# TensorE's counts of logits, shared products and attended rows behind a drain, and variance's root ahead of the weights' low halves

## The reference

```python
xn = _layernorm(x, axis=-1)
s = _L0_attn_ref(xn, Wq, Wk, Wv, Wo)         # attention over the 256 features of a batch, not over its rows
g = _silu(_L0_ffn_ref(xn, gate_weight, w1, w2, w3, sw1, sw2, sw3))
x = x + s * g
```

## Time and profile before

| what | value |
|---|---|
| time, median of 3 runs | 685.56 us (684.07 to 687.75) |
| the profiled execution's own time | 691.99 us |
| its span | 690.2 us |
| PE busy | 548.6 us (79%), 4095 matmul passes |
| DVE, ACT, POOL busy | 472.2, 359.1, 383.4 us (68%, 52%, 56%) |
| TensorE's granted clock, mean | 0.922 |

### The profile page before, as it was taken

One profiled execution on the slowest core, in us unless ns is written; L12 is line 12 of the kernel. 1 busy time (PEld: TensorE's weight loads), 2 busy tenths in 40 slices (PEclk: granted clock), 3 DMA queues, 4 the chain that ended last, 5 costly groups with the idle time before them and its releaser, 6 DMA issues.

```text
span 690.2 us, 14473 instructions
## 1 busy us (share of the span) xinstructions
PE 548.6 (79%) x4095; PEld 446.7 (65%) x4095; DVE 472.2 (68%) x1443; ACT 359.1 (52%) x606; POOL 383.4 (56%) x402
## 2 busy tenths in 40 slices
PE   7789696979697978437999889888888889888830
PEld 6566575756576765326999777777777777677620
DVE  6968687877788877722454567667677667667765
ACT  5546464546464644224655656556556556556421
POOL 1156667676666766753003556556565556565662
PEclk9889798998898999868999999999999999999975
DMA  9999996858393532754888888888888988888764
GB/s 320 416 354 347 366 334 227 285 214 298 130 334 113 207 117 91 230 150 122 201 217 262 290 280 283 280 280 285 290 272 292 279 279 267 290 276 286 226 198 141
DMA packets 111288, 174.80 MB, mean 253 GB/s; under 512 B 25072, under 2 KB 68848, under 8 KB 110320
## 3 DMA queue, kind: packets, MB, share of 16 engines
q1 hardware_dynamic: 87280, 108.29, 47.4%
q0 software_dynamic: 18432, 50.36, 23.2%
q10 hardware_dynamic: 5504, 15.24, 6.4%
HBM read 78.41 MB, written 92.27 MB: 247 GB/s over the span
## 4 chain that ended last, share of the span: by engine, by line
PE 53%; DVE 21%; issue 15%; another core or an unknown queue 6%; ACT 4%; DMA 1%; DVEq 0%; SPq 0%; ACTq 0%
PE ps L835 17%; PE ps L857 8%; PE ps L726 7%; PE ps L710 6%; PE ps L818 6%; PE ps L718 4%; DVE sw L1133 3%; PE ps L845 3%; PE ps L732 2%; DVE w_all L1050 2%; DVE work L1152 2%; DVE work L1159 1%; DVE stats L877 1%; DVE early L1141 1%
## 5 line engine op out<-in xcount | busy, mean ns | idle before, releaser
L508 POOL DMA_INDIRECT early<-slots_d,slot_at x192 | 186.6, 972 | 178.0 <-DMA slots_d<-early 56.6
L487 POOL DMA_INDIRECT slots_d<-early,slot_at x96 | 96.9, 1009 | 75.0 <-issue 25.7
L487 POOL DMA_INDIRECT slots_d<-work,slot_at x96 | 97.7, 1018 | 45.1 <-issue 26.5
L835 PE MATMUL ps<-w_all,xnT 128*128 x798 | 102.9, 275 | 15.9 <-issue 13.6
L835 PEld LDWEIGHTS ps<-w_all,xnT 128*128 128x128 f16 x798 | 71.4, 98 | 36.3 <-issue 24.6
L647 ACT ACTIVATE xnT<-ps 128x1024 f16<-128x1024 f16 x67 | 68.8, 1029 | 46.6 <-PE ps L818 28.0
L668 ACT ACTIVATE early<-ps 128x512 f32<-128x512 f32 x112 | 67.3, 602 | 46.6 <-remote 30.8
L818 PE MATMUL ps<-ident,work 128*128 128x128 f16 x796 | 66.7, 222 | 24.9 <-issue 24.8
L1159 DVE CAST work<-ps 128x256 f16<-128x256 f32 x75 | 31.6, 422 | 75.0 <-remote 45.0
L1133 DVE SCALAR_TENSOR_TENSOR sw<-early,wk,sw 128x256 f32<-128x256 f32 x160 | 77.7, 486 | 3.5
L818 PEld LDWEIGHTS ps<-ident,work 128*128 128x128 f16 x796 | 54.6, 99 | 28.8 <-issue 26.4
(11 more groups left out here) (164 smaller groups left out, 989.4 us busy)
## 6 DMA issues: line engine op xcount, KB each, us to landing
slots_d<-early SPq DMA_DIRECT2D x112, 256.0 KB
work<-slots_d SPq DMA_DIRECT2D x100, 256.0 KB
slots_d<-pad SPq DMA_DIRECT2D x7, 3072.0 KB
w_all<-in_wexp ACTq DMA_DIRECT2D x7, 1536.0 KB
slots_d<-work SPq DMA_DIRECT2D x1, 5120.0 KB, 19.2
s_all<-in_x SPq DMA_DIRECT2D x8, 512.0 KB, 6.3
ysh_d<-work ACTq DMA_DIRECT2D x8, 512.0 KB
early<-ysh_d SPq DMA_DIRECT2D x32, 128.0 KB
```

Source lines behind the costliest of these rows:

```text
L487: pool.indirect_dma_start(slots_d[:, :], bass.IndirectOffsetOnAxis(ap=slot_at[:, at:at + 1], axis=0), split[b % XN_RING][:, t, :], None).t ...
L508: pool.indirect_dma_start(gath[:, at % GATH_RING, :], None, slots_d[:, :], bass.IndirectOffsetOnAxis(ap=slot_at[:, rank_of(at):rank_of(at) ...
L835: mm = pe.matmul(ps[:, 5 + p % 2, h * 2 * I:(h + 1) * 2 * I], turned_x(p)[:, x_low * HC + k, h * P:(h + 1) * P], w16[:, bass.ds(at + (w_lo ...
```

## The change

Two edits. In `gate` and `half_by_tile` the count no longer hangs on the last matmul: TensorE gets a drain behind it, and the drain raises the count. `product`, `shared_up`, `turn`, `gram`, `count` and the experts' matmuls keep theirs on the matmul. And DVE computes `spread_root(b + 2)` and `moved_mean` ahead of `low_weights(b - 1)` instead of behind it. What let_pass waits for stays as it is.

```diff
@@ gate(b)
                     for c in range(HC):
-                        mm = pe.matmul(ps[:, 4, t * E:(t + 1) * E], xnT[b % 2][:, c, t * P:(t + 1) * P],
+                        pe.matmul(ps[:, 4, t * E:(t + 1) * E], xnT[b % 2][:, c, t * P:(t + 1) * P],
                                        g_w[:, c, :], start=(c == 0), stop=(c == HC - 1))
-                mm.then_inc(s_lg_ps, 1)
+                pe.drain().then_inc(s_lg_ps, 1)
@@ half_by_tile(n, bank, lhs, rhs, done)
-                        mm = pe.matmul(ps[:, bank + n, t * H:(t + 1) * H], lhs[:, k, at:at + P], rhs[:, k, :],
-                                       start=(k == 0), stop=(k == HC - 1))
-                mm.then_inc(done, 1)
+                        pe.matmul(ps[:, bank + n, t * H:(t + 1) * H], lhs[:, k, at:at + P], rhs[:, k, :],
+                                  start=(k == 0), stop=(k == HC - 1))
+                pe.drain().then_inc(done, 1)
@@ DVE's batch(b)
                 route(b + 1)
                 split_low(b + 1)
-                if b >= 1:
-                    low_weights(b - 1)
                 if b + 2 < B:
                     spread_root(b + 2)
                     moved_mean()
+                if b >= 1:
+                    low_weights(b - 1)
                 place(b + 1)
                 weigh(b + 1)
```

## The result

The four executions of the changed kernel took 699.39, 702.66, 709.24 and 714.82 us (median 705.95), those of the kernel before 686.65 in the median. The longest of the four is a slow execution and stays out of the ratio, which is 1.0213, 95% interval [1.0162, 1.0264], or 14.6 us slower, about 701 us. The forecast was 679.5 us and a gain; the second rival (the drain is held, TensorE stands; 703 us) is what came.

The account below looks back on a forecast made before the run. TensorE idles 60 us in the batches, partly through counts held while POOL issues indirect DMAs. 691.99 + 7.0 - 7.4 - 1.5 - 3.7 - 0.6 = 685.8, 6.2 us less; for the median 679.5 us, range 671 to 700.

Parts of the forecast that it names:

- the second rival: Drains are held like counts and TensorE stands behind attended halves and second shared product; 703 us, chance 0.31.
- what they bring, if their counts aren't held: Gains from the drains' counts passing freely: 7.4 us at L925, 1.5 at L598, 3.7 from POOL's stops.
- the first rival: The forecast itself: the drains' counts pass freely; 679.5 us, own range 671 to 682, chance 0.46.
- matmuls go on meanwhile, so the array isn't stuck: Argument for free drain counts: TensorE keeps running matmuls while engines waiting for its counts are held.
- L925: DVE's first routing instruction, waiting for the logits' count in three batches; the whole 7.4 us wait taken as gain.
- L598: ACT's eviction of the shared products; of 16.1 us of waits only 1.5 us taken as gain.
- POOL's stops at L726: POOL's 7 stops for L726's count, 11.1 us in all; a third, 3.7 us (0 to 11.1), taken as gain.
- 20 exposed drains: Drains behind attended halves (16) and second shared products (4), 0.35 us each on TensorE: 7.0 us lost (5.2 to 12).
- 16 drains are covered: Drains behind logits and first shared product cost nothing, since TensorE waits for the row weights anyway (6.44, 3.10 us).
- Variance's root: DVE's root ahead of the low halves: L527's wait falls from 17.8 to about 4 us; gain 0.6 us (0 to 3.9).
- 5.6 us of lost gains: Point from which the second rival decides: 5.6 of the 12.6 us that free counts bring fail to come.
- The third: Rival: the hold only moves, to plain counts of r and m; only L925's gain stays; 684.6 us, chance 0.23.

Follow-up runs that it names:

- set 3: One chip, kernel before 696.98 us: changed kernel again 1.0148; it without scatters 0.9352; counts on matmuls plus drains raising nothing 1.0373; changed kernel with earlier POOL stop 1.0109.
- set 4: Kernel before without scatters 0.9370, changed kernel without scatters 0.9373; kernel before with earlier POOL stop 1.0028; changed kernel without POOL's stops 1.1670.
- three part-by-part runs: Kernel before with drains behind one kind of product only: logits 1.0064, shared products 1.0075, attended halves 1.0142.

## Why the prediction was wrong

**The step that failed** is the one under *what they bring, if their counts aren't held*, and the choice of the first rival (0.46) over the second (0.31) on which it rests. The argument for it was that "matmuls go on meanwhile, so the array isn't stuck". The observation is right; the conclusion does not follow. PE goes on because nothing behind a held count asks for it. A drain asks. It put the stands at nothing; they are 46.1 us ahead of L726 in one profile of the changed kernel and 27.6 in the other. The drains without a count in set 3 show that the hold is in the drain and not in what it raises, and set 4 shows that without scatters there is nothing to wait for. What exactly is late in the matmuls' completion isn't shown: a late end and a late report of it look alike in these rows, as the prediction said.

The prediction also weighed the Trainium skill: "PSUM — Partial Sum Buffer", section "Engine vs sequencer instructions", calls the drain a barrier that waits until the engine is fully idle. By this rule read so, TensorE stands, and the traces agree: 46.1 us in 13 waits ahead of L726, up to 5.8 us. The rule doesn't say why an engine whose last matmul is shown as ended 4.5 us ago isn't idle, and no run here does.

**The gains, term by term** (in brackets the profile of set 3). L925: 7.4 us to win; its wait grew to 18.2 us (13.8). L598: 1.5 to win; the wait went from 16.1 to 17.2 us (11.0), so one profile has it longer and one shorter. POOL's stops at L726: 11.1 us, to fall by a third; POOL's waits for that count are 42.0 us (24.0). Of the 12.6 us nothing shows in the time.

**The drain's price.** 20 exposed drains at 0.35 us, 7.0 us, were too many rather than too few: without scatters the difference is -1.0 us in set 4, uncertain by some 3 us, and +0.6 on the faster chip. With scatters the term is another one, stands of 2 to 6 us, once 10, and the lower clock behind them.

**"16 drains are covered"** was right of a drain of 0.35 us and wrong of a held one. The gate's drains became the dearest stands, 24.4 us; the cover paid back 22.4 - 7.0 = 15.4 us of them at L710 (19.3 and 15.3 us in the profile of set 3).

**Variance's root**: the wait of L527 fell to 6.0 us (about 4 forecast) and the time by nothing: 1.0003. The reading that another count, not ACT, came last fits: in the profile of the moved root L610 itself stands 5.1 us for a "remote" count. The term of 0.6 us can't be told from none. That term was left out where the prediction has the second rival decide from 5.6 us of lost gains; with it that point is 6.2.

**The rivals.** The second had 703 us, measured about 701, and the nearness is luck: the price was put together from other places. It had POOL's seven stops at L726 as the price, no stand behind the gate, and the lower clock only in the upper bound of a drain's 0.35 us. The third (the hold moves to plain counts) came in part: L602 and L610, which it named, waited less (9.9 to 4.8 us, and 3.6 to none), and L949 and L568 more (2.9 to 14.5, and none to 13.1). What that cost isn't shown.

**What stays open**: what a hold waits for between TensorE and POOL's indirect DMAs, and whether it is their issuing or their writes, since all runs take away both (traffic alone isn't it: the faster chip moves 270 GB/s in its batches with scatters and holds nothing, the kernel before 233); why some end while POOL issues; why counts with drains behind them (23 us) are dearer than drains with counts (10 us in the same set); why four chips have holds and one none.

## What to carry to other kernels

When a completion shows late in a trace, ask what instruction will wait for the same completion before you put a barrier in front of it: a barrier turns a reader's wait, which the producer can run past, into a stand of the producer, and the stand costs clock as well. A cover pays for the idle time alone: in the second profile TensorE was idle no longer than before, and 11 us went to slower matmuls. Two profiles of one program gave two different splits of the loss, so read a second before you believe one. A wait called covered is covered up to the length of its cover at its usual duration; price it once more at the worst duration that the trace shows for its kind (here 5 us and once 10, not 0.35). And measure the cost of an instruction with its suspected neighbour removed, in both kernels: the twins without scatters settled in one comparison what three part-by-part runs could not.

## What the runs showed of the hardware

- On the chips with holds, with scatters under way, TensorE's counts and its drains, also those that raise nothing, come 2 to 6 us late, at one place 10 (the last batch's drain; 13 for a count at that place in the kernel before, 284.68 to 297.83) and up to 12 behind the gate without stops; in the batches without scatters no matmul group behind a drain stood more than 0.3 us for "issue". The gate's drains take 6.7 and 4.6 us in the median with scatters and 2.3 without.
- After a halt of POOL they come 1.6 us behind the end of its last indirect DMA (190.90 to 192.53 above); in the kernel without stops 2.9 us behind it (206.25 to 209.16), and there the gate's drain is also let go without a halt, four times after 4.0 to 4.1 us. The stops in `let_pass` are worth 97 us to the kernel before.
- Leaving out the scatters takes 43 us of 689 on one chip and 2.7 of 590 on another; on the latter no hold was seen. Four of the five chips ran the kernel before at 689 to 697 us. Without scatters the batches take as long on either (the experts begin at 267.4 and 267.3 us), with scatters 42 us longer on the former (312.2 against 270.2). The rest of the difference between the chips lies in the experts (378.0 us from their first matmul on, against 319.1 on the fast chip). A result on this question from one chip need not hold on the next.
